# Second attention written out in 64 stages: queries projected with the weights stationary, rotary embedding on turned queries with halves swapped by DMA, probabilities normalised on GpSimd

## What is computed

```
h = rmsnorm(hidden, ln1_w)
q = rope((h @ Wq).reshape(B, S, 32, 128)); k = rope((h @ Wk).reshape(B, S, 4, 128)); v = (h @ Wv)...
scores = q k^T / sqrt(128), causal; attn = softmax(scores)
x = hidden + (attn @ repeat(v, 8)) @ Wo
...
_rope: x1, x2 = split(x, 2); concatenate([x1*cos - x2*sin, x1*sin + x2*cos])
```

## Time and profile before

| what | value |
|---|---|
| median of 3 runs | 1058.37 us |
| lowest and highest run | 1055.94 and 1061.75 us |
| span of the profiled execution | 1054.1 us |
| attention 2: from the first join work to the turns of the second norm | about 184 to 725 us |
| attention 2, one iteration in the loop | 30.4 us |
| busy in 283 to 313.4 us: PE, DVE, ACT, POOL | 29.73, 25.16, 19.59, 15.49 us |

### The profile page before, as it was taken

One profiled execution on the slowest core, in us unless ns is written; L12 is line 12 of the kernel. 1 busy time (PEld: TensorE's weight loads), 2 busy tenths in 40 slices (PEclk: granted clock), 3 DMA queues, 4 the chain that ended last, 5 costly groups with the idle time before them and its releaser, 6 DMA issues. The chain is left out here.

```text
span 1054.1 us, 21008 instructions
## 1 busy us (share of the span) xinstructions
PE 946.4 (90%) x6296; PEld 833.8 (79%) x6296; DVE 675.7 (64%) x1542; ACT 580.1 (55%) x1571; POOL 477.6 (45%) x428
## 2 busy tenths in 40 slices
PE   3799998478899999999999999987899999999994
PEld 2699998367888888888888888887677778777774
DVE  7356666657888888888888888884343343344435
ACT  4788886545566665666666666554333333333333
POOL 5533333365455545455545444401455444445552
PEclk9899999688999999999999999998999999999997
DMA  5001000200000300030000001000433323333221
GB/s 197 15 2 41 20 21 1 90 22 1 1 21 1 109 20 20 20 109 20 19 0 20 21 20 35 1 1 16 128 93 98 103 93 102 104 104 101 90 87 40
DMA packets 41846, 52.96 MB, mean 50 GB/s; under 512 B 3888, under 2 KB 34224, under 8 KB 41808
## 3 DMA queue, kind: packets, MB, share of 16 engines
q1 hardware_dynamic: 40720, 51.44, 15.0%
q10 hardware_dynamic: 1088, 1.05, 0.3%
HBM read 41.86 MB, written 1.18 MB: 41 GB/s over the span
## 5 line engine op out<-in xcount | busy, mean ns | idle before, releaser
L1849 DVE TENSOR_TENSOR moe_hidden<-banks,moe_scaled 128x512 f32<-128x512 f32 x66 | 45.7, 692 | 183.5 <-POOL moe_scaled L1811 183.5
L1811 POOL TENSOR_TENSOR moe_scaled<-moe_silu,moe_share 128x512 f32<-128x512 f32 x66 | 85.9, 1301 | 159.2 <-ACT moe_silu L1746 150.4
L1255 POOL TENSOR_TENSOR b_sin_part<-b_raw,rope_sb 128x512 f32<-128x512 f32 (+1 forms) x96 | 114.7, 1195 | 93.7 <-ACT b_raw L1211 93.7
L1746 ACT ACTIVATE moe_silu<-banks 128x512 f32<-128x512 f32 x66 | 39.5, 598 | 196.3 <-PE banks L75 196.3
L1266 POOL TENSOR_TENSOR b_q_row<-b_cos_part,b_sin_part 128x512 f32<-128x512 f32 x64 | 82.0, 1281 | 75.8 <-DVE b_cos_part L1230 68.9
L551 ACT ACTIVATE b_prob<-banks,b_negmax 128x128 f32<-128x128 f32 (+1 forms) x256 | 104.5, 426 | 16.9 <-DVE b_negmax L592 16.9
L592 DVE TENSOR_REDUCE b_negmax<-banks 128x1 f32<-128x128 f32 (+1 forms) x256 | 76.6, 351 | 54.4 <-PE banks L488 49.8
L608 DVE TENSOR_SCALAR b_prob<-b_prob,b_rsum 128x128 f32<-128x128 f32 (+1 forms) x256 | 106.5, 477 | 2.3
L617 POOL TENSOR_TENSOR a_prob<-a_prob,a_rsum 128x256 f32<-128x256 f32 x64 | 51.6, 826 | 85.7 <-DVE a_rsum L599 85.7
L73 PE MATMUL banks<-b_w,b_ot 128*128 (+1 forms) x256 | 77.9, 304 | 12.5 <-DVE b_ot L1163 12.5
L488 PE MATMUL banks<-mask,ident 128*128 128x128 bf16 x384 | 88.6, 234 | 0.0
(11 more groups left out here) (227 smaller groups left out, 3238.6 us busy)
## 6 DMA issues: line engine op xcount, KB each, us to landing
moe_share<-gates SPq DMA_DIRECT2D x32, 512.0 KB, 3.7
b_src_t<-act_t SPq DMA_DIRECT2D x13, 512.0 KB, 2.9
b_w_raw<-in_b_wq SPq DMA_DIRECT2D x4, 1024.0 KB, 5.7
b_w_raw<-in_b_wo SPq DMA_DIRECT2D x4, 1024.0 KB, 7.7
a_src_t<-act_t SPq DMA_DIRECT2D x5, 512.0 KB, 2.9
moe_w_raw<-in_wg SPq DMA_DIRECT2D x16, 128.0 KB, 2.2
moe_w_raw<-in_wu SPq DMA_DIRECT2D x16, 128.0 KB, 2.2
moe_w_raw<-in_wd SPq DMA_DIRECT2D x16, 128.0 KB, 2.3
```

Of the source, the lines that this page charges most:

```text
L1255: nc.gpsimd.tensor_tensor(out, x, factor, ALU.mult).then_inc(self.sin_ready, 1)
L1811: nc.gpsimd.tensor_tensor(scaled[n][:], silu[n][:], share[par][:, n * half:(n + 1) * half], ALU.mult).then_inc(scaled_done, 1)
```

## The change

Attention 2 no longer uses the loop, the units or `src_t`: `slots` writes 64 stages P out with constant addresses. `pe_queries` makes the queries of one pair of heads in place of a Q unit: 12 matmuls with 128 columns of the weights stationary (one head) and the 256 tokens moving, so that the result already has the head's 128 numbers on the partitions. The four transposes of L1107 are gone. In a slot it makes pair P+3. ACT copies the bank to `raw`. SP then swaps the two halves of 64 partitions with two transfers, `raw` to `swp`. DVE multiplies `raw` by the turned cosine table (`dve_cos`), POOL multiplies `swp` by the sine table and adds (`pool_rotate`), ACT and DVE make high and low part from the SBUF sum (`act_queries`, `dve_queries`), where before they read PSUM. Keys and values have their own bank and tiles. POOL normalises the probabilities, and DVE only takes the reciprocals. `prepare` turns the two tables for queries with four transposes and one ACT copy.

```diff
+            pe.wait_ge(rope_loaded, 16)
+            pe.wait_ge(w_lo, 1)
+            for k in range(2):
+                for t in range(NTT):
+                    last = nc.tensor.transpose(w_bank(0)[:, k, t * PART:(t + 1) * PART], m.rope[:, k, t, :],
+                                               m.ident[:])
...
+            act.wait_ge(rope_turned, 1)
+            nc.scalar.activation(m.rope_t[:], w_bank(0), ACT.Copy)
...
-    ITS, UNITS = B_ITS, 7
-    schedule = ((KV0, KV1), (Q00, Q01), (KT,), (Q10, Q11))
+    ITS = B_ITS
+    STAGES = PAIRS * B_ITS
+    POOL_NORMALISES = True
+    KV_AT = {0: KV0, 1: KV1, 3: KT}
+    ROPE_AT = {1: KV0, 2: KV1}
...
+    def pe_queries(self, pe, P):
+        nc, it, p = self.m.nc, P // PAIRS, P % PAIRS
+        wait(pe, self.w_ready, 4 * (it // NB) + 3)
+        if P >= 2:
+            wait(pe, self.raw_ready, P)
+        for h in range(2):
+            out = self.q_bank(P)[:, h * SEQ:(h + 1) * SEQ]
+            for c in range(NC):
+                at = c * B_QKV + (2 * p + h) * DH
+                last = three(nc, out, self.w_at(it, 0, at, DH), self.w_at(it, 1, at, DH),
+                             self.src(it, 0, c, 0, SEQ), self.src(it, 1, c, 0, SEQ), c == 0, c == NC - 1)
+        last.then_inc(self.q_full, 1)
+    def sp_swap(self, sp, P):
+        wait(sp, self.raw_ready, P + 1)
+        wait(sp, self.q_added, P - 1)
+        half = DH // 2
+        for to, of in ((0, half), (half, 0)):
+            sp.dma_start(self.swp[to:to + half, P % 2, :], self.raw[of:of + half, P % 2, :],
+                         ).then_inc(self.swapped[P % 2], 16)
+    def dve_cos(self, dve, P):
+        wait(dve, self.raw_ready, P + 1)
+        wait(dve, self.qt_ready, P - 1)
+        self.m.nc.vector.tensor_tensor(self.pairs_of(self.cos_part, P), self.pairs_of(self.raw, P),
+                                       self.q_table(0), ALU.mult).then_inc(self.cos_ready, 1)
+    def pool_rotate(self, pool, P):
+        wait(pool, self.swapped[P % 2], self.SWAPPED * (P // 2 + 1))
+        sin = self.pairs_of(self.swp, P)
+        nc.gpsimd.tensor_tensor(sin, sin, self.q_table(1), ALU.mult).then_inc(self.sin_ready, 1)
+        wait(pool, self.cos_ready, P + 1)
+        wait(pool, self.sin_ready, P + 1)
+        nc.gpsimd.tensor_tensor(total, total, self.swp[:, P % 2, :], ALU.add).then_inc(self.q_added, 1)
+    def act_queries(self, act, P):
+        wait(act, self.q_added, P + 1)
+        wait(act, self.s_full, 2 * (P - PAIRS + 1))
...
+    def slot_pe(self, pe, P):
+        it, p = P // PAIRS, P % PAIRS
+        if self.runs(P):
+            self.pe_scores(pe, *self.at(P))
+        if it + 1 < self.ITS and p in self.KV_AT:
+            self.pe_kv(pe, it + 1, self.KV_AT[p])
+        if self.runs(P - 5):
+            self.pe_project(pe, *self.at(P - 5))
+        if self.runs(P - 4):
+            self.pe_values(pe, *self.at(P - 4))
+        if self.runs(P + 3):
+            self.pe_queries(pe, P + 3)
+        if self.runs(P - 2):
+            self.pe_prob_t(pe, (P - 2) % PAIRS, P - 2)
...
+            for P in range(self.STAGES):
+                slot = P - 3
+                if slot > 0 and slot % (PAIRS * NB) == 0 and slot // (PAIRS * NB) < KV - 1:
+                    load_weights(slot // (PAIRS * NB) + 1)
+                self.sp_swap(sp, P)
```

More of the change, by code:

```diff
@@ L698, in __init__ @@
         sb, sem = self.sb, self.sem
+        self.src_t = sb("src_t", [PART, SLOT], F32R)
+        self.qt = sb("qt", [PART, 2, 2, 2 * SEQ], F32R)
         rest = m.b_w[:, 2 * B_W:4 * B_W]
@@ L1079, in pe_unit @@
-            last.then_inc(self.unit_full, 1)
+                last = nc.tensor.transpose(bank[:, t * PART:(t + 1) * PART], self.k_row[:, t, :], self.m.ident[:])
+            last.then_inc(self.kv_full, 1)
             return
-        self.wait_src(pe, it)
+        t = u
         wait(pe, self.w_ready, 4 * (it // NB) + 3)
[L1084 to L1090, removed]
@@ L1091, in pe_unit @@
-        for c in range(NC):
[L1092 to L1109, removed]
+        if u == self.KV0:
+            wait(pe, self.kt_ready, it)
+        elif it:
+            wait(pe, self.k_raw_ready, NTT * it + 1)
@@ new lines, in keys, with values, act_values @@
+    def keys(self, it, part, n):
+        at = (it % 2) * (2 * SEQ) + part * SEQ
+        return self.kt[:, at:at + n]
+    def values(self, it, t, n):
+        at = (it % 2) * (NTT * DH) + t * DH
+        return self.v_row[:, at:at + n * DH]
+    def act_values(self, act, it):
+        wait(act, self.v_raw, NTT * (it + 1))
+        wait(act, self.pv_done, PAIRS * it)
+        self.m.nc.scalar.activation(self.v[:, 0, :, :].rearrange("p t n -> p (t n)"),
+                                    self.values(it, 0, NTT), ACT.Copy).then_inc(self.v_hi, 1)
@@ L1177, in dve_values @@
[L1177 to L1214, removed]
@@ new lines, in slot_pool, with slots @@
+    def slot_pool(self, pool, P):
+        it, p = P // PAIRS, P % PAIRS
+        if self.runs(P - 1):
+            self.pool_normalise(pool, (P - 1) % PAIRS, P - 1)
+        if self.runs(P + 2):
+            self.pool_rotate(pool, P + 2)
+        if it + 1 < self.ITS and p in self.ROPE_AT:
+            self.pool_kv(pool, it + 1, self.ROPE_AT[p])
+        if p == PAIRS - 1 and self.more_weights(it):
+            self.pool_weights(pool, it)
+    TAIL = 7
+    def slots(self, eng, slot, plan):
+        for P in range(self.STAGES + self.TAIL):
+            slot(eng, P)
+            for stage, b in plan.get(P - self.STAGES, ()):
+                stage(b)
@@ L1398, in _, with work @@
-            for k in range(self.DRAIN, self.TAIL):
-                self.tail(plan, k)
+            self.slots(pe, self.slot_pe, {
+                4: ((turn_h2, 0), (turn_h2, 1), (turn_h2, 2), (route, 0)),
+                5: ((turn_h2, 3), (route, 1)), 6: ((route, 2),)})
         @block.scalar
         def _(act):
-            def work(s, units=behind(act, self.act_unit)):
-                units(s)
+            def work(s):
+                if s == 3:
+                    self.act_kv(act, 0, self.KV0)
+                    self.act_kv(act, 0, self.KV1)
```

398 lines of the change are left out of this document (218 added, 180 removed).

## The result

The changed kernel takes 1040.74 us (median of 4 runs, 1039.79 to 1046.13) against 1059.17 for the kernel before on the same chip: a ratio of 0.9842, with a 95% interval of 0.9809 to 0.9874. It is faster, but by 17 to 18 us, not by 40. The profiled executions differ by 14.9 us of span.

A forecast was written before the change was run, and what follows sets the result against it. PE bounded the old kernel; afterwards a POOL-DVE-ACT loop would, at 28.2 us an iteration until the last four. Savings of 22, 10, 8 and 2 less 1.5 make 40.5 us, giving 1018 us, range 995 to 1043.

The forecast's parts named there:

- PE's work: Steady part of attention 2: from 30.4 to about 26.9 us an iteration if PE stays the limit.
- The doubled weight loads: Query matmuls on PE: weight loads double, but nothing added, as outputs' matmuls already load new weights at the 0.12 us pace.
- The 10 us ahead of the steady part: Before iteration 2: 8 us less in iterations 0 and 1, 2 us less ahead of the first scores.
- The swap: Exchange of raw's halves: lands 4 us after raw, hidden with 2 us to spare, except behind two weight loads.
- the loop is the longer one in iterations 0 to 11: Attention 2: POOL, DVE and ACT's chain takes 28.4 us an iteration against PE's 26.9, some 1.5 longer.
- The loop: Chain from reciprocal through POOL's normalisation, product and sum, ACT and DVE to the next reciprocal: 24.1 us an iteration before additions.
- the keys as 0.4 us of delay: POOL's keys in slots 1 and 2 keep `dve_queries` waiting about 0.4 us each, 0.8 an iteration.
- the weights in slot 3: POOL's weight split (2.69 us) delays `dve_queries` in slot 3, adding 1.9 to 2.0 us to an iteration.
- Swaps behind weights: Two of 64 swaps queue behind a weight load on SP: 1.5 us added for both (0 to 10).
- The 4.41 us of the earlier trace: Four DVE `tensor_scalar` took this beside POOL's weight split, 1.01 without; read as DVE and POOL excluding each other on SBUF.
- PE stays the bound: Rival, chance 0.22: hops and collisions smaller than taken, so PE sets the pace; 60 us less, 998 us.
- The loop costs more: Rival, chance 0.15: collisions cost whole POOL instructions or PE waits for outputs; 29.5 to 31 us an iteration, 1036 to 1055.

The follow-up runs named there:

- the early split: Changed kernel with key transposes moved behind the value matmuls and POOL's weight split at the start of slot 3 instead of its end: 1013.72 us, ratio 0.9594.
- the fastest version: Changed kernel with key transposes later, POOL rotating keys first, weight split at the start of slot 3, two weight loads issued by ACT: 1005.31 us, ratio 0.9516.
- the small edit in the kernel before: Kernel before with one part of the change alone, POOL normalising the probabilities of attention 2: 1037.37 us, ratio 0.9814.
- keys' wait put back: The fastest version with key transposes again directly behind slot 3's scores and POOL's keys again behind its rotation: 1037.64 us, ratio 0.9813.
- late keys: Changed kernel with slot 3's key transposes moved behind the value matmuls, with the same move on ACT and DVE: 1021.39 us, ratio 0.9655.

## Why the prediction was right and wrong

Right: PE's work. The slots of 7.0, 7.0, 6.3 and 6.5 are 7.07, 7.07, 6.34 and 6.56 where nothing waits, 27.04 in all for the 26.9 forecast. The doubled weight loads cost nothing. The 10 us ahead of the steady part came as forecast, although PE waits 3.9 us for the keys in slot 3 of the first iteration there, which the sum did not have. The swap takes 2.3 us and is covered. `prepare` cost nothing: attention 1 starts at 24.79 in place of 24.83.

Wrong, the step that failed: "the loop is the longer one in iterations 0 to 11". The loop was followed to one exit only, the scores' wait for b_qt. The same phases (normalisation 4 to 5 us into POOL's slot, then 4.4 us to the sum, then 1.1 us for the keys) put the end of the keys 3.5 us behind the start of PE's scores in slot 3, and PE comes to the key transposes after 2 us. The prediction counted the keys as 0.4 us of delay for `dve_queries` and never asked who waits for them. This wait is what the faster slots ran into: of the 3.4 us that PE's work would have saved in an iteration, it took 1.5 to 2.3, and 1.6 more where the clock fell.

As a term of its own the loop was oversized: in 300 to 600 us PE never waits for b_qt, and POOL waits 1.8 us a slot for the reciprocal, so there was slack in the loop where the prediction had none. Only with the early split did a chain through POOL and DVE show, at 28.2 us, the size forecast but through another exit.

Wrong in size: the weights in slot 3. The prediction charged them 1.9 us of loop each, and they cost no PE time there (DVE's cosine product at 391.61 took 3.19 us beside such a split, and PE did not wait for it). What they cost is a wait of PE for the third quarter in slots 12, 28 and 44, with its clock, 10 us, which had no term. In the changed kernel it is hidden behind the keys' wait but for 0.9 us in slot 28. Swaps behind weights were taken at 1.5 us. They are 5 once the keys' wait is gone, and in the changed kernel slots 19 and 35 are no longer than others with the same stall.

A reading was off too. The 4.41 us of the earlier trace rows stand beside two instructions of POOL, the sum at 268.02 (1.29 us) and the split at 269.64 (2.69), and not beside the split alone. They are `tensor_scalar`, with one tensor as input, and so no case of the two SBUF inputs that the prediction made of them. The cosine product above is one, 3.19 us beside a split in place of 0.69.

The rival "PE stays the bound" was right about the mechanism without the waits. The rival "The loop costs more" has the measured time in its 1036 to 1055, but by luck: it had PE wait for b_qt or for outputs, and in 300 to 600 us PE waits for neither. None of the rivals had the wait that decided.

The traces split the loss roughly. From slot 7 to slot 59 the slots 3 of the changed kernel are 41.7 us longer than 14 x 6.56. Of this 26.5 us are PE's waits for b_k_row. The other 15.2 are about what eight falls of the clock cost, seven of 3.4 us and one of 6.8, at half the pace. That a kernel without the stalls has no falls from 250 us to the end of the attention is shown (the fastest version, the one with the early split, and the small edit in the kernel before). Why the clock falls behind some stalls of 1.5 us (324.5, 355) and not behind others (385.05) stays open.

## What to carry to other kernels

When work moves to another engine, list everything that this engine hands over and put each item's new time of completion against the slot in which its reader stands. The critical hand-over is not always the large one: two instructions of 0.46 us on 128 columns decided here. Test the parts alone: one small part of this change gave its whole gain, and the rest paid only when two waits, each visible in one row of the waits, had been removed and a third halved by a few lines. A stall of PE can cost twice, since the clock may fall behind it.

## What the runs showed of the hardware

The clock of PE falls to the lower level for 3.4 us, sometimes 6.8, behind single stalls of 1.5 to 3.8 us in stages that are busy 90% and more all the same. With the keys' wait it did so behind 8 of 14 stalls (changed kernel) and 5 of 15 (keys' wait put back), and from 250 us on it never fell in the versions without such stalls.

A swap that SP issues behind 2.25 MB of weights comes late: POOL waits 2.8 and 3.0 us for it, and PE loses 5.1 us for both loads together (late keys). With the loads issued by ACT, POOL waits 1.3 us each and PE loses 2.5, and ACT itself stands still for some 2 us at its issues. So the other queue halves the loss and does not remove it. What is left was not taken apart.
